# Last expert tile turned by TensorE instead of a DMA transpose, and a scatter's waits in another order

## The reference

```python
x = x + xattn(layernorm(x), ctx, ctx, mask, Wq, Wk, Wv, Wo, bo)
# ffn, on layernorm(x):
scores = sigmoid(x_flat @ gate.T + bias)
top_scores, selected = top_k(scores, 2)          # weights divided by their sum
for e in range(9):
    h = silu(x_flat @ ew1[e].T) * (x_flat @ ew3[e].T)
    out = out + cw[:, e:e+1] * (h @ ew2[e].T)
x = x + out
```

## Time and profile before

| | |
|---|---|
| median of 3 runs | 438.3 us (436.89 to 439.7) |
| the profiled execution | 441.96 us |
| its span, first to last instruction | 440.1 us |
| TensorE busy | 409.6 us, 93% of the span |
| VectorE, ScalarE, GpSimd busy | 66%, 55%, 59% |

### The profile page before, as it was taken

The page is one execution under the profiler, slowest core; times in us unless marked ns, Lnnn a source line. Parts: engine busy times, 40 slices in busy tenths (PEclk is TensorE's granted clock), DMA queues, the critical chain, the costliest instruction groups (busy, mean ns, idle before and its releaser), DMA issues.

```text
span 440.1 us, 10125 instructions
## 1 busy us (share of the span) xinstructions
PE 409.6 (93%) x3165; PEld 307.4 (70%) x3165; DVE 289.7 (66%) x703; ACT 242.5 (55%) x423; POOL 258.2 (59%) x201
## 2 busy tenths in 40 slices
PE   8899899999999998679998999999999999999971
PEld 8676677777777876655765777777777777777750
DVE  1768799999999899987878655444444444444310
ACT  3769799698888843236743444444444444444320
POOL 6436979988999955152145454555555555554241
PEclk9999999999999999988998999999999999999996
DMA  8983355566566443038678699999999999999660
GB/s 269 377 280 114 104 160 167 172 183 193 158 183 188 145 133 115 27 112 242 121 153 151 113 125 136 148 141 130 144 149 139 139 139 139 125 154 139 109 106 12
DMA packets 107680, 66.38 MB, mean 151 GB/s; under 512 B 82416, under 2 KB 100720, under 8 KB 107632
## 3 DMA queue, kind: packets, MB, share of 16 engines
q1 hardware_dynamic: 99952, 55.25, 57.6%
q0 software_dynamic: 7680, 10.49, 17.8%
HBM read 36.23 MB, written 9.96 MB: 105 GB/s over the span
## 4 chain that ended last, share of the span: by engine, by line
PE 73%; DVE 11%; DMA 4%; ACT 4%; issue 3%; POOL 2%; POOLq 0%; DVEq 0%; ACTq 0%; SPq 0%
PE ps L779 29%; PE ps L792 15%; PE ps L624 9%; PE ps L599 9%; PE ps L612 3%; DMA stage<-in_wt 2%; PE ps L510 2%; DMA work<-work 2%; PE ps L594 1%; DVE work L1111 1%; DVE work L1105 1%; DVE w_all L1169 1%; PE ps L522 1%; PE ps L568 1%; POOL w_all L1531 1%
## 5 line engine op out<-in xcount | busy, mean ns | idle before, releaser
L779 PE MATMUL ps<-w_all,work 128*128 x960 | 152.5, 316 | 1.6 <-ACT work L988 1.1
L779 PEld LDWEIGHTS ps<-w_all,work 128*128 128x128 f16 x960 | 94.7, 99 | 50.3 <-issue 2.7
L1606 POOL DMA_INDIRECT out_rows<-work,idx_all x40 | 63.7, 1592 | 100.4 <-ACT work L999 79.0
L792 PE MATMUL ps<-w_all,work 128*128 x680 | 83.0, 278 | 4.6 <-DMA work<-work 4.6
L1441 DVE SCALAR_TENSOR_TENSOR work<-ps,work 128x352 f32<-128x352 f32 x80 | 41.4, 523 | 68.5 <-PE ps L779 66.7
L792 PEld LDWEIGHTS ps<-w_all,work 128*128 128x128 f16 x680 | 67.2, 99 | 16.6 <-issue 5.3
L1585 POOL DMA_INDIRECT work<-xn_rows,idx_all x40 | 54.0, 1349 | 32.4 <-DVE work L1434 11.8
L1531 POOL TENSOR_TENSOR w_all<-stage,w_all 128x1088 f16<-128x1088 f32 x28 | 63.2, 2257 | 5.0 <-ACT w_all L867 5.0
L994 ACT ACTIVATE work<-work 128x704 f16<-128x704 f32 x40 | 31.6, 789 | 61.3 <-DVE work L1441 59.3
L988 ACT ACTIVATE work<-ps 128x352 f32<-128x352 f32 x80 | 36.1, 461 | 38.8 <-PE ps L779 37.3
L599 PE MATMUL ps<-w_all 128*128 128x462 f16 (+1 forms) x288 | 57.4, 336 | 0.0
(11 more groups left out here) (148 smaller groups left out, 532.9 us busy)
## 6 DMA issues: line engine op xcount, KB each, us to landing
stage<-in_wt SPq DMA_DIRECT2D x36, 544.0 KB, 4.1
work<-in_x SPq DMA_DIRECT2D x30, 128.0 KB, 3.6
out_rows<-work SPq DMA_DIRECT2D x18, 128.0 KB, 4.4
xn_rows<-work SPq DMA_DIRECT2D x18, 128.0 KB, 4.0
w_all<-in_x SPq DMA_DIRECT2D x1, 1536.0 KB, 13.7
work<-work SPq DMA_TRANSPOSE x79
w_all<-in_wk SPq DMA_DIRECT2D x2, 512.0 KB, 4.9
w_all<-in_wq SPq DMA_DIRECT2D x4, 256.0 KB, 7.2
```

Of the source, the lines that this page charges most:

```text
L779: mm = pe.matmul(ps[:, c, 0:half], xt[:, t % 2, block, :], weights(wbase + off, half), start=(k == 0 and n == 0), stop=(k == KD - 1 and n ...
L792: mm = pe.matmul(ps[:, Y_BANKS[t % 2], 0:D], ht[:, t % 2, block, :], weights(wbase + (pl * WC + W13C + c * D), D), start=(c == 0 and n == ...
L1606: pool.indirect_dma_start(out=acc, out_offset=bass.IndirectOffsetOnAxis(ap=idx_all[:, t:t + 1], axis=0), in_=yb[:, t % 2], in_offset=None, ...
```

## The change

It has two parts.

First, the last tile (`T_END` = 39) no longer goes through `h_high`, `h_low` and `turn_hidden`. In step 39, behind `down(37)` and ahead of `down(38)`, PE turns the float32 product `sg` itself, in six transposes into the PSUM banks 5 and 6 (`end_turn`). ACT copies the turned blocks to float16 straight into `ht` (`end_high`, three instructions), and DVE subtracts that from PSUM for the low part (`end_low`, two small memsets and three subtractions). The low part of the last, 64 wide block gets a buffer of its own (`end_lo`, a piece of `xt`), so `down(39)` has 18 matmuls and waits for ACT and DVE instead of a DMA.

Second, in every scatter the wait for the tile (`y_ok`) now stands last, just ahead of the DMA, behind the waits for the earlier scatters.

```diff
+        end_mm, endh_ok, endl_ok = sem("end_mm"), sem("endh_ok"), sem("endl_ok")
...
-        Y_BANKS = (7, 4)
+        Y_BANKS, END_BANKS, T_END = (7, 4), (5, 6), NF - 1
+        end_lo = xt[:, T_END % 2, 0, :]
...
             def turn_hidden(t):
+                if t == T_END:
+                    return
...
             def down(t, wbase):
                 at_least(pe, y_ok, t - 1)
-                pe.wait_ge(ht_in[t % 2], (t // 2) * 16 + 16)
+                if t == T_END:
+                    pe.wait_ge(endh_ok, 3)
+                    pe.wait_ge(endl_ok, 2)
+                else:
+                    pe.wait_ge(ht_in[t % 2], (t // 2) * 16 + 16)
                 for c in range(HC):
                     terms = ((c, 0), (HC + c, 0), (c, 1)) if c < HC - 1 else ((c, 0), (c, 1))
+                    if t == T_END and c == HC - 1:
+                        terms = ((c, 0), (None, 0), (c, 1))
...
+            def end_turn():
+                pe.wait_ge(h_ok, 2 * NF)
+                for g, blocks in enumerate((range(4), range(4, HC))):
+                    for c in blocks:
+                        w = min(P, HID - c * P)
+                        mm = pe.transpose(ps[0:w, END_BANKS[g], (c % 4) * P:(c % 4 + 1) * P],
+                                          sg[:, T_END % 2, c * P:c * P + w], con[:, C_ID:C_ID + P])
+                    mm.then_inc(end_mm, 1)
...
                 if s >= 2:
                     down(s - 2, eids.pop(s - 2) * (2 * WC))
+                if s == T_END:
+                    end_turn()
...
+            def end_high(g):
+                act.wait_ge(end_mm, g + 1)
+                src = ps[:, END_BANKS[g], :].rearrange("p (c t) -> p c t", t=P)
+                if g == 0:
+                    act.activation(ht[:, T_END % 2, 0:4, :], src, ACT.Copy).then_inc(endh_ok, 1)
+                else:
+                    act.activation(ht[:, T_END % 2, 4, :], src[:, 0, :], ACT.Copy).then_inc(endh_ok, 1)
+                    act.activation(ht[0:P // 2, T_END % 2, 5, :], src[0:P // 2, 1, :], ACT.Copy).then_inc(endh_ok, 1)
...
+                if n == T_END + 1:
+                    weigh(n - 3)
+                    for g in range(2):
+                        end_high(g)
+                    return
...
+            def end_low(g):
+                src = ps[:, END_BANKS[g], :].rearrange("p (c t) -> p c t", t=P)
+                hi = ht[:, T_END % 2]
+                if g == 0:
+                    dve.wait_ge(end_mm, 1)
+                    dve.memset(hi[P // 2:P, 5, :], 0.0)
+                    dve.memset(end_lo[P // 2:P, :], 0.0)
+                    dve.wait_ge(endh_ok, 1)
+                    dve.tensor_tensor(hi[:, HC:HC + 4, :], src, hi[:, 0:4, :], ALU.subtract).then_inc(endl_ok, 1)
+                else:
+                    dve.wait_ge(endh_ok, 3)
+                    dve.tensor_tensor(hi[:, HC + 4, :], src[:, 0, :], hi[:, 4, :], ALU.subtract)
+                    dve.tensor_tensor(end_lo[0:P // 2, :], src[0:P // 2, 1, :], hi[0:P // 2, 5, :], ALU.subtract).then_inc(endl_ok, 1)
...
             def scatter(t, more):
                 landed = (t + 1) // 2 * 16
                 at_least(pool, s_out[t % 2], (t // 2) * 16)
-                pool.wait_ge(y_ok, t + 1)
                 if more is None:
                     at_least(pool, s_out[1 - t % 2], landed)
                 else:
                     pool.wait_ge(s_out[1 - t % 2], more + (landed - 16))
                     pool.sem_inc(clear, 1)
+                pool.wait_ge(y_ok, t + 1)
                 pool.indirect_dma_start(out=acc, ...)
```

More of the change, by code:

```diff
@@ L787, in down @@
                 at_least(pe, y_ok, t - 1)
-                pe.wait_ge(ht_in[t % 2], (t // 2) * 16 + 16)
+                if t == T_END:
[3 more added lines that the diff above has]
+                    pe.wait_ge(ht_in[t % 2], (t // 2) * 16 + 16)
                 for c in range(HC):
                     terms = ((c, 0), (HC + c, 0), (c, 1)) if c < HC - 1 else ((c, 0), (c, 1))
+                    if t == T_END and c == HC - 1:
+                        terms = ((c, 0), (None, 0), (c, 1))
                     for n, (block, pl) in enumerate(terms):
-                        mm = pe.matmul(ps[:, Y_BANKS[t % 2], 0:D], ht[:, t % 2, block, :],
-                                       weights(wbase + (pl * WC + W13C + c * D), D),
-                                       start=(c == 0 and n == 0), stop=(c == HC - 1 and n == 1))
+                        lhs = end_lo if block is None else ht[:, t % 2, block, :]
+                        mm = pe.matmul(ps[:, Y_BANKS[t % 2], 0:D], lhs, weights(wbase + (pl * WC + W13C + c * D), D),
+                                       start=(c == 0 and n == 0), stop=(c == HC - 1 and n == len(terms) - 1))
                 mm.then_inc(w2_mm, 1)
+            def end_turn():
[6 more added lines that the diff above has]
+                    mm.then_inc(end_mm, 1)
             def expert(t):
@@ L1449, in h_low @@
                                   ALU.subtract).then_inc(hl_ok, 1)
+            def end_low(g):
[11 more added lines that the diff above has]
+                    dve.tensor_tensor(end_lo[0:P // 2, :], src[0:P // 2, 1, :], hi[0:P // 2, 5, :], ALU.subtract).then_inc(endl_ok, 1)
             def fstep(n):
+                if n == T_END + 1:
+                    for g in range(2):
+                        end_low(g)
+                    return
                 if onf(n, 1):
```

## The result

| | before | after |
|---|---|---|
| median (lowest to highest), 10 runs each | 439.91 us (436.89 to 442.35) | 436.44 us (435.18 to 437.49) |
| the profiled execution | 441.96 us | 436.6 us |
| its span | 440.1 us | 434.8 us |
| start of `down(37)` to the last scatter's start | 12.54 us | 8.31 us |
| `down(39)` | 17 matmuls, 3.69 us | 18 matmuls, 2.1 us |

After takes 0.9921 of the time of before (95% interval 0.9896 to 0.9947): 3.5 us less, between 2.3 and 4.6. The forecast was 434.0 with a range from 432.4 to 436.2; the median lies 0.2 us above that range. The gain forecast, 4.3 us, lies inside the measured interval. The median of before is 439.91 in ten runs and was 438.3 in the three that the forecast started from.

The account below looks back on a forecast made before the run. TensorE's matmuls bind the steady loop, a serial chain the end. Turn and wait order start the last scatter at 428.7 instead of 432.97, 4.3 us less, with the 7.1 us tail unchanged: median 434.0 us, range 432.4 to 436.2.

Parts of the forecast that it names:

- The base: Whole kernel: the median before the change that the forecast started from, 438.3 us in three runs.
- The term for the clock: Ahead of and in down(39): TensorE saves 2.62 us idle and 1.75 low clock, less 0.69 and 0.11: 3.6 us.
- the case of a fallen clock: In the changed kernel down(39) takes 3.7 us instead of 2.05, or the split is late: 434.8 us; chance 0.08.
- The turn: Behind down(37): six TensorE transposes take 0.69 us, down(38) hides the split, down(39) ends at 427.05 instead of 430.62.
- The tie between the landing and the last matmul: Ahead of tile 39's weigh: tile 37's scatter lands at 427.0, down(39) ends at 427.05.
- The order of the waits: Scatters of tiles 3 to 39 but 14: the hand-over passes before the tile comes, start 0.28 us behind it.
- the wait doesn't hide the hand-over: At the scatters, the hand-over still follows the tile wait; last start about 429.3, 3.7 us less: 434.6 us; chance 0.12.
- Long or short hand-over: Last scatter behind tile 37's landing: long 1.78 us, 434.0, chance 0.48; short 0.92 us, 433.2, chance 0.22.
- Slower through the first tiles: First expert tiles: new TensorE gaps, 3.7 us each; one gives about 437.7, chance 0.06; two 441.4, chance 0.04.

Follow-up runs that it names:

- the implied wait: The changed kernel without the last scatter's own wait for tile 37's scatter, which tile 39's weigh already waits for: 435.69 us, ratio 0.9887; repeated 436.46 us, 0.9911.

## Why the prediction was wrong, and where it was right

Two numbers failed, and both lie outside the reading of the changed end.

**The base.** "The profiled execution would come to 441.96 - 4.3 = 437.7 (span 435.8), the median to 434.0" took 438.3, a median of three, as where the kernel stands. In the ten runs of the comparison it was 439.91, and medians of 29, 11 and 24 further ones gave 440.07, 440.53 and 439.42. Single runs go from 436.89 to 444.78. That error is 1.6 us: with the same gain the forecast would have been 435.6.

**The term for the clock.** "That is 3.6 us, made up of the idle 2.62 and the 1.75 of low clock" set the 1.75 in full. In the execution that was read it was true: 17 matmuls took 3.69. It holds in only three of six executions of that kernel. Where the clock falls it costs 3.69 - 2.03 = 1.7 us, and over the six executions the end is 12.54 - 11.70 = 0.8 us shorter than in the one that was read. So the mean gain is 11.70 - 8.34 = 3.4 us and not 4.3; against the single executions of before it is either 2.5 or 4.2. The range had no room for it, since the case of a fallen clock was thought of for the changed kernel only, never that the kernel before might keep its clock. The statement that the clock was still 1.00 through the rest, and low when work came, rested on one execution; even there the clock fell 0.1 us behind the start of `down(39)`.

The two sum up: 434.0 + 1.6 + 0.8 = 436.4, measured 436.44. That it closes so well is partly luck, since the second term is a mean over six executions. The two may also overlap: an execution that keeps its clock is 1.7 us shorter, and nothing tells how many of the first three runs were such.

**The turn** was right step by step. Six transposes took 0.65 us (0.69 forecast). ScalarE's three copies took 0.60, 0.27 and 0.26 (0.59 and under 0.39), VectorE's subtractions 0.69, 0.28 and 0.27 (0.66, 0.28, 0.28). The split ended about 0.25 us before it was wanted (0.15 forecast). There is no rest, PEclk is 1.00, and `down(39)` takes 2.1. The tie between the landing and the last matmul came too, both at about 425.83, with a landing 3.77 us behind the scatter's start, where 3.75 was taken.

**The order of the waits** was right as well. The tile wait that is left alone behind the register step is held by the DMA instruction, and the hand-over has passed when the tile comes: 0.27 to 0.30 behind the weigh in 32 of the 35 tiles from 4 to 38, where it was mostly 0.94 to 0.99. The three others are tile 14 (0.83, a step of its own, as forecast) and tiles 16 and 25 (1.30 and 1.12), which wait for the scatter ahead. Tile 1 went the other way, 0.28 to 0.80, so 0.5 later, where the forecast named 0.6. The case "the wait doesn't hide the hand-over" falls with it. The Trainium skill's sentence in DMA: Bandwidth & Descriptors (anatomy of one DMA, gpsimd path) is that any semaphore wait happens on the issuing sequencer before dispatch. Read as the prediction read it, with the whole hand-over behind the wait, it doesn't agree with these runs: they are 0.7 us sooner in each such scatter. Where dispatch itself lies no trace here shows.

**Long or short hand-over.** The long one came true, with 1.42 us of issue for the last scatter. The forecast had the start 428.7 - 420.43 = 8.3 us behind `down(37)`, and the trace has 8.31. That the landing of tile 37's scatter starts it is shown by taking that wait away: 0.75 us less. That the tile itself isn't late is shown by moving it 0.36 later at no cost.

**Slower through the first tiles**: no trace shows it. The start of `down(5)` varies by 6.8 us over all traces, and both orders have early and late ones. The forecast also called the DMA engines full there. They were not: their busy share through that transpose (232.57 to 237.96 us) was 0.85, in the steady loop 1.06.

The best version made is the changed kernel with the implied wait, with an end of 7.56. It is 0.8 us shorter in both of its traces, less than the times can tell (0.9911 against 0.9927, with intervals that overlap).

## What to carry to other kernels

Before a term rests on a granted clock that fell, look at it in several executions; where only one is at hand, write the term as a range from nothing to its full size, and let the range of the forecast follow. Where a DMA waits for several things, see to it that the DMA instruction itself holds the wait for the one that comes last, and leave out every wait that the late one implies: what stands ahead holds back the hand-over. Here the instruction held that wait when it was the only one behind a register step, or the first of several plain ones. As the last of several plain ones it became a step of its own, so look in the profile which it is. And take the level of a forecast from as many runs as there are: here three runs missed the median by 1.6 us, nearly half of what the change is worth.

## What the runs showed of the hardware that was not expected

- Nearly the same rest of TensorE, 2.60 to 2.63 us on the same instruction of the same program, is followed by the low clock in three executions (17 matmuls in 3.64 to 3.69 us, PEclk 0.53 to 0.55, close to the lower level of 1.2 GHz) and by full clock in three (2.03 us, PEclk 1.00). With a rest of 2.69 us one kernel showed 2.87: about 1.0 us at full clock, then 0.50. With a rest of 1.19 us the one trace at hand shows 2.03.
- The last scatter has 1.4 us of issue ahead of it where the ones of the loop hand over in 0.6 to 0.7. It stays with a value read behind it, with four more in front, and with another transfer behind it. With the wait for the landing gone the scatter starts sooner. The cause stays open.
- Which wait the scatter instruction holds depends on what stands between the waits: the one behind the `sem_inc` in 36 tiles, the first of several plain ones in tile 1 of the kernel before (0.28 us behind the weigh), not the last of several plain ones in tiles 1 and 14 of the changed kernel (0.80 and 0.83).
- A scatter that holds its tile wait itself starts 0.28 us behind the tile in the loop, but 0.46 to 0.47 behind it as the last one, when its longer hand-over has begun early enough.
